# A DeepFM and CIN kernel: two more fields of tile 1 are looked up on chip in tile 0, and the last tile is transposed ahead of a layer of the tile before it

## What is computed

```python
emb = embed_table[f_ix, x_idx]                      # n, 26, 16
lin1 = w1_table[f_ix, x_idx].sum(axis=1, keepdims=True) + w1_bias
s = emb.sum(axis=1)
fm = 0.5 * ((s * s).sum(-1) - (emb * emb).sum(axis=(1, 2)))[:, None]
h = relu(emb.reshape(n, F * D) @ mlp_w1 + mlp_b1)
h = relu(h @ mlp_w2 + mlp_b2)
mlp_out = h @ mlp_w3 + mlp_b3
x0 = last = emb.transpose(0, 2, 1)
feats = []
for W in (cin_w0, cin_w1, cin_w2):
    last = einsum('ndl,ndf,klf->ndk', last, x0, W)
    feats.append(last)
cin = concatenate(feats, axis=-1).sum(axis=1) @ lin_w + lin_b
return lin1 + fm + mlp_out + cin
```

## Time and profile before

| | before |
|---|---|
| runs, us | 497.53, 497.66, 498.18 (median 497.66) |
| profiled execution, us | 496.48 |
| its span, us | 494.7 |
| mean granted clock of PE | 0.991 |
| busy share of the span | PE 92%, DVE 84%, ACT 74%, POOL 70% |
| gathers on POOL | 360 |
| look-ups | 56 |

### The profile page before, as it was taken

The page is one execution under the profiler, slowest core; times in us unless marked ns, Lnnn a source line. Parts: engine busy times, 40 slices in busy tenths (PEclk is TensorE's granted clock), DMA queues, the critical chain, the costliest instruction groups (busy, mean ns, idle before and its releaser), DMA issues.

```text
span 494.7 us, 6809 instructions
## 1 busy us (share of the span) xinstructions
PE 453.1 (92%) x2171; PEld 383.0 (77%) x2171; DVE 414.2 (84%) x861; ACT 368.2 (74%) x726; POOL 345.5 (70%) x365
## 2 busy tenths in 40 slices
PE   0988986899999999999999999999999999999898
PEld 0985764788888888888888888888877887878666
DVE  6163358999999999999999999999989989989676
ACT  0163499678787887888787878787887878687694
POOL 5777778777777777777777777777777777777000
PEclk9999998899999999999999999999999999999999
DMA  7963794222222222222222222222222222222000
GB/s 159 209 168 27 110 201 113 38 7 8 8 9 7 7 9 7 10 7 8 8 8 7 8 8 8 7 8 8 8 8 9 7 9 7 8 8 7 3 0 2
DMA packets 21522, 15.59 MB, mean 32 GB/s; under 512 B 12802, under 2 KB 19823, under 8 KB 21359
## 3 DMA queue, kind: packets, MB, share of 16 engines
q0 software_dynamic: 11520, 3.16, 18.6%
q1 hardware_dynamic: 6962, 9.99, 8.2%
q10 hardware_dynamic: 3005, 2.01, 2.0%
HBM read 14.92 MB, written 0.21 MB: 31 GB/s over the span
## 4 chain that ended last, share of the span: by engine, by line
POOL 65%; issue 22%; ACT 5%; PE 4%; DVE 3%; DMA 1%; POOLq 0%; DVEq 0%
POOL emb L499 65%; ACT ps_s L598 2%; ACT z_hi L591 2%; ACT z_hi L593 1%; DVE z_lo L796 1%; PE ps_q L1096 1%; PE ps_y L1127 1%; DVE xt L789 0%; DMA idx_raw<-x_idx 0%; PE ps_q L1097 0%; PE ps_q L1098 0%; DMA emb<-rows,idx_raw 0%; ACT room_a L597 0%; DVE sums L822 0%; DVE ps_y L935 0%
## 5 line engine op out<-in xcount | busy, mean ns | idle before, releaser
L499 POOL DMA_INDIRECT emb<-rows,idx_raw x360 | 345.1, 959 | 112.2 <-issue 109.4
L796 DVE TENSOR_TENSOR z_lo<-ps_s,z_hi 128x512 fp32r<-128x512 f32 (+1 forms) x192 | 131.4, 684 | 35.0 <-ACT ps_s L598 34.4
L591 ACT ACTIVATE z_hi<-ps_s 128x512 fp32r<-128x512 f32 (+1 forms) x192 | 114.4, 596 | 40.3 <-PE ps_s L1083 39.9
L598 ACT ACTIVATE ps_s<-ps_s 128x512 f32<-128x512 f32 (+1 forms) x192 | 113.9, 593 | 0.8
L1182 PE MATMUL ps_y<-look_hi,one_hot 128*128 128x442 f32 x224 | 82.1, 366 | 6.4 <-DVE one_hot L924 5.7
L1083 PE MATMUL ps_s<-xt,pick 128*128 128x512 f32 (+1 forms) x192 | 77.2, 405 | 9.3 <-ACT x_two L584 6.6
L1096 PE MATMUL ps_q<-z_lo,zw_hi 128*127 128x512 f32 (+1 forms) x192 | 79.6, 415 | 6.6 <-DVE z_lo L796 4.8
L1183 PE MATMUL ps_y<-look_lo,one_hot 128*128 128x442 f32 x224 | 79.4, 356 | 0.0
L1098 PE MATMUL ps_q<-z_hi,zw_hi 128*127 128x512 f32 (+1 forms) x192 | 75.9, 395 | 0.0
L1097 PE MATMUL ps_q<-z_hi,zw_lo 128*127 128x512 f32 (+1 forms) x192 | 75.8, 395 | 0.0
L1083 PEld LDWEIGHTS ps_s<-xt,pick 128*128 128x128 f32 (+1 forms) x192 | 35.6, 186 | 23.4 <-DVE z_lo L796 11.2
(11 more groups left out here) (187 smaller groups left out, 687.3 us busy)
## 6 DMA issues: line engine op xcount, KB each, us to landing
emb<-rows,idx_raw POOLq DMA_INDIRECT x360, 3.0
w_space<-rows SPq DMA_DIRECT2D x2, 728.9 KB
m_space<-rows SPq DMA_DIRECT2D x2, 728.9 KB
w_space<-key_scratch SPq DMA_DIRECT2D x1, 1408.0 KB, 8.6
w<-cin_w SPq DMA_DIRECT2D x2, 416.0 KB, 6.7
w<-cin_w ACTq DMA_DIRECT2D x2, 416.0 KB, 9.3
w_space<-cin_w SPq DMA_DIRECT2D x2, 416.0 KB, 8.4
w_space<-cin_w ACTq DMA_DIRECT2D x2, 416.0 KB, 8.2
```

The source lines that it names most:

```text
L499: pool.indirect_dma_start(emb[t % EMB][:, f, :], None, rows, bass.IndirectOffsetOnAxis(row_ix[:, t, f:f + 1], 0)).then_inc(gathered[t] if ...
L591: act.activation(z_hi[0:k, c, :], ps[0:k, :], ACT.Square)
L598: act.activation(ps[0:k, :], ps[0:k, :], ACT.Square).then_inc(hi_ready, 1)
L796: z = dve.tensor_tensor(z_lo[0:k, u % NC, :], ps, z_hi[0:k, u % NC, :].bitcast(F32), ALU.subtract)
```

## The change

Two of the empty slots are filled. Fields 22 and 23 of tile 1 are no longer gathered but looked up in slots 0 and 1 of tile 0 (`AHEAD = 2`), so tile 0 has four look-ups and tile 1 24 gathers. Tile 0 gets dictionaries of its own (`ROWS_0`, `KEYS_0`, `PICKED_0`), and the low parts of the tables are made one unit after the high ones in place of two. The copy of tile 1 waits for its two look-ups. The keys of tiles 1 and 2 come in with two loads. All later look-ups keep their slots.

Besides, `fold` moves from the end of `start_tile` to unit 4 of tiles 1 to 14, and `sum_products` from unit 3 to unit 6. In the step into tile 15, ACT makes the first part of the last copy ahead of the squares of unit 11; PE transposes ahead of the second layer of tile 14, and the eight filling matmuls go; DVE's `start_last` gets another order, in which the read of the second layer (`hidden2`) and `add_third` come behind unit 0 of tile 15. The diff, cut to what is spoken of; the parts belong, in order, to the constants, SP, POOL, ACT, DVE and PE:

```diff
-LATER = 2
+AHEAD = 2
...
-        key_first = sb("key_first", [P, LOOKS, P], F16)
+        key_first = sb("key_first", [P, AHEAD + LOOKS, P], F16)
...
         def looks(t):
-            return LOOKS if FIRST_LOOK <= t < T else 0
+            return LOOKS if FIRST_LOOK <= t < T else AHEAD if t == FIRST_LOOK - 1 else 0
 
         def look_no(t, i):
-            return LOOKS * (t - FIRST_LOOK) + i
+            return AHEAD + LOOKS * (t - FIRST_LOOK) + i if t >= FIRST_LOOK else i
 
         def look_at(t, slot):
-            n = LOOKS * t + slot - LATER
-            return (FIRST_LOOK + n // LOOKS, n % LOOKS) if 0 <= n < look_no(T, 0) else None
+            n = LOOKS * t + slot
+            if n < AHEAD:
+                return (FIRST_LOOK - 1, n)
+            m = n - AHEAD
+            return (FIRST_LOOK + m // LOOKS, m % LOOKS) if n < look_no(T, 0) else None
 
         def looked_by(t):
-            return min(max(LOOKS * t + 1 - LATER, 0), look_no(T, 0))
+            return min(LOOKS * t + 2, look_no(T, 0))
...
         ROWS = {0: 0, 3: 1, 6: 2, 9: 3}
         KEYS = {3: 1, 6: 2, 8: 3}
         PICKED = {3: 0, 6: 1, 9: 2}
+        ROWS_0 = {5: 0, 7: 1, 9: 2, 11: 3}
+        KEYS_0 = {3: 0, 5: 1, 7: 2, 9: 3}
+        PICKED_0 = {7: 0, 9: 1, 11: 2}
...
-        WARM, WARM_FIRST, WARM_LAST = 8, 4, (4, 4)
+        WARM, WARM_FIRST = 8, 4
...
-            sp.dma_start(key_first[:].rearrange("p i n -> p (i n)"),
-                         key_dram[LOOKS * FIRST_LOOK:LOOKS * (FIRST_LOOK + 1), :].rearrange(
-                             "r n -> (r n)").partition_broadcast(P)).then_inc(keys_first_in, 16)
+            for t, i0, i1 in ((FIRST_LOOK - 1, 0, AHEAD), (FIRST_LOOK, AHEAD, AHEAD + LOOKS)):
+                sp.dma_start(key_first[:, i0:i1, :].rearrange("p i n -> p (i n)"),
+                             key_dram[LOOKS * t:LOOKS * t + i1 - i0, :].rearrange(
+                                 "r n -> (r n)").partition_broadcast(P)).then_inc(keys_first_in, 16)
...
-                for f in range(F - looks(t)):
+                for f in [*range(F - LOOKS), *range(F - LOOKS + looks(t), F)]:
                     pool.indirect_dma_start(emb[t % EMB][:, f, :], None, rows,
...
                 if looks(t):
-                    act.wait_ge(looked, look_no(t, LOOKS))
+                    act.wait_ge(looked, look_no(t, looks(t)))
...
+                    if u == NU - 1 and t + 1 == T - 1:
+                        copy_last_early()
                     square(t, u)
                     if u == NU - 1 and t + 1 == T - 1:
-                        copy_last_early()
                         copy_last_late()
...
                     if u % NC == 2 and q:
                         add_product(t, q)
+                    if u == 4 and 0 < t < T - 1:
+                        fold(t - 1)
                     if u == 7:
                         hidden1_low(t)
-                    if t == 0 and u - 2 in LOOK_SPLIT:
-                        look_low(LOOK_SPLIT[u - 2])
-                    if u in PICKED and look_at(t, PICKED[u]):
-                        pick_row(*look_at(t, PICKED[u]))
-                    if u in KEYS and look_at(t, KEYS[u]):
-                        keys_to_one_hot(*look_at(t, KEYS[u]))
+                    slots = PICKED if t else PICKED_0
+                    if u in slots and look_at(t, slots[u]):
+                        pick_row(*look_at(t, slots[u]))
+                    if t == 0 and u - 1 in LOOK_SPLIT:
+                        look_low(LOOK_SPLIT[u - 1])
+                    slots = KEYS if t else KEYS_0
+                    if u in slots and look_at(t, slots[u]):
+                        keys_to_one_hot(*look_at(t, slots[u]))
 
             def start_last():
                 t = T - 1
+                times_third(t - 1)
                 times_left(t - 1, NQ - 1)
-                times_third(t - 1)
-                add_third(t - 1)
-                hidden2(t - 1)
                 x_low(t, 0)
                 x_low(t, 1)
                 z_low(t, 0)
+                hidden2(t - 1)
+                add_third(t - 1)
                 z_low(t, 1)
                 add_product(t - 1, NQ - 1)
                 z_low(t, 2)
...
                 add_product(t - 1, NQ - 1)
-                fold(t - 1)
...
-                    if u == 3 and t:
+                    if u == 6 and t:
                         sum_products(t - 1)
...
-                    if u in ROWS and look_at(t, ROWS[u]):
-                        look_rows(*look_at(t, ROWS[u]))
+                    slots = ROWS if t else ROWS_0
+                    if u in slots and look_at(t, slots[u]):
+                        look_rows(*look_at(t, slots[u]))
...
                 else:
+                    x_all(after)
                     hidden2(t)
-                    wait_for_bank(after, 1)
-                    free = s_bank(after, 0)
-                    keep_warm(free, WARM_LAST[0])
-                    x_all(after)
-                    keep_warm(free, WARM_LAST[1])
                     picked(after, 0)
                     picked(after, 1)
                     hidden1_whole(after)
```

More of the change, by code:

```diff
@@ L914, in keys_to_one_hot @@
             def keys_to_one_hot(t, i):
-                if i == 0 and t == FIRST_LOOK:
-                    dve.wait_ge(keys_first_in, 16)
+                if i == 0 and t == FIRST_LOOK - 1:
+                    dve.wait_ge(keys_first_in, 16 * 2)
                 elif i == 0 and t in (FIRST_LOOK + 1, FIRST_LOOK + 3):
@@ L919, in keys_to_one_hot @@
                 n = look_no(t, i)
-                keys = key_first[:, i:i + 1, :] if t == FIRST_LOOK else key_row[:, t - FIRST_LOOK - 1, i:i + 1, :]
+                keys = key_first[:, n:n + 1, :] if t <= FIRST_LOOK else key_row[:, t - FIRST_LOOK - 1, i:i + 1, :]
                 if n >= 2:
@@ L1173, in look_rows @@
                 n = look_no(t, i)
-                if n < LOOKS:
+                if t <= FIRST_LOOK:
                     pe.wait_ge(look_lo_ready, i + 1)
```

## The result

The changed kernel took 493.95 us (median of 4 runs, 493.86 to 494.42), the kernel before beside it 497.60 us (496.67 to 498.18): ratio 0.993, 95% interval 0.9917 to 0.9942. It is faster, by 0.3 to 0.7%, and both times lie under the predicted range of 495.9 to 501.0.

The account below looks back on a forecast made before the run. Two lines, DVE with ACT and POOL's gathers, were taken to bound the kernel, the later setting tile 14. Terms +0.2 - 0.1 + 1.2 = +1.3 us on the median 497.66 gave 498.9; range 495.9 to 501.0.

Parts of the forecast that it names:

- Tiles 1 to 13: Moving the fold and row sum in these tiles changes nothing: 0, bounds -0.05 and +0.05 us a tile.
- the compute line: DVE with ACT, setting the 26.34 us tile pace; predicted to bring tile 14's copy at 433.1, later than the gathers.
- by tile 14's copy: Start of tile 14's copy: +0.2 us against before, what the gathers save being spent in tile 0.
- the time from there to the end: From tile 14's copy on: -0.1 us for tile 14 and the last step together, +1.2 for the clock.
- putting the sum on a median: The +1.3 us sum was added to the median 497.66, not to the profiled execution of 496.48, giving 498.9.
- The gather line: POOL's gathers up to tile 14: two fewer, 2.5 us earlier; range 5.3 earlier to 0.3 later.
- Tile 0: Two added look-ups delay DVE's second x_low of tile 1 by 4.4 us, with stalls of 1.2 and 1.9; bounds +1.3, +7.3.
- the sign: Trace sign that the forecast is right: tile 2's copy starts near 117.0 us.
- Tile 14: PE no longer waits for comparisons behind the fold, so ACT's squares from unit 7 come 0.65 us earlier; bounds 0, -1.
- The step into tile 15: New order gains 2.2 us, lost again waiting for DVE's second-layer read; -0.1 us together with tile 14.
- The clock: PE's new 3.07 us gap before tile 15's first layer brings half clock: +1.2 us, range 0 to +2.4.
- Rival (2): Tile 0 takes the look-ups without the two stalls, +1.3; gathers decide tile 14, 2.5 us earlier: 496.3 us, chance 0.15.

Follow-up runs that it names:

- e1: Changed kernel with the fold and PE's row sum back at their old places: 498.27 us, ratio 1.0023 to the kernel before.
- e5: Changed kernel with the step into the last tile as in the kernel before, filling matmuls included: 493.38 us, ratio 0.9923 to the kernel before.
- e11: Changed kernel with the fold behind unit 3 in place of unit 4, row sum still at unit 6: 497.16 us, ratio 1.001 to the kernel before.
- e9: Changed kernel measured once more, nothing altered, as base for later runs: 495.39 us, ratio 0.9974 to the kernel before.
- e3: Changed kernel with the fold behind unit 3 and the row sum at unit 3: 497.31 us, ratio 0.9999 to the kernel before.
- e4: Changed kernel without the two look-ups of tile 1, the rest as changed: 498.77 us, ratio 1.0031 to the kernel before.
- e6: Changed kernel with DVE's read of tile 14's second layer ahead of unit 0 of tile 15: 491.82 us, ratio 0.9899 to the kernel before.
- e8: Changed kernel with four more reductions of the fold's input on DVE, unused, in tiles 3 and 4: 498.92 us, ratio 1.004 to the kernel before.
- e2: Changed kernel with the fold alone back at its old place, row sum at its new one: 499.91 us, ratio 1.006 to the kernel before.

## Why the prediction was wrong

**The step that failed is "Tiles 1 to 13", "I take 0, bounds -0.05 and +0.05 a tile".** Measured: -0.26 a tile. Its reason, "the same work stands between the same two waits", looked at DVE's two long waits alone. What was missing is that PE's comparisons stood behind the fold in every tile, not only in tile 14, where the prediction saw PE's idle 0.41 us for them and credited 0.65 us; and that a fold right behind its input starts 0.13 us late. About half of the 0.26 us is that start, the other half are DVE's short waits for ACT ahead of units 8 and 11, which the new place ends. Over the twelve tiles from copy 2 to copy 14 this is 3.1 us, and tile 1 gains 0.6 more: enough to turn which line comes later.

**The kernel nearest to the one that the prediction described is e1.** With the fold at its old place the compute line brings copy 14 at 434.10 without a wait (predicted 433.1). That its time of 498.27 us lies near the predicted 498.9 is partly luck: its first tiles came 1.3 us late, and its clock did not fall, for which the prediction had 1.2 us; the two about cancel.

**How the miss adds up.** The forecast was 5 us too high: 2.6 us by tile 14's copy (+0.2 predicted, -2.44 measured), 0.8 by the time from there to the end (+1.1 and +0.34), and 1.6 by putting the sum on a median that lay 1.2 us over the profiled execution before and 0.5 under it afterwards.

The other steps, one by one:
- The gather line, -2.5: it moved from 432.93 to 430.49, -2.44. That the number fits is partly luck. In it lie two things that nearly cancel: no gather of tile 0 takes 2.3 us any more in this execution (the longest 1.35), 1.4 us less in all, and the usual distance of two gathers is 1.258 us where it was 1.251, 1.6 us more in all. The first is a matter of the execution: e5 and e11, whose tile 0 is the same, have a gather of 2.79 us beside the third table split, the nine other profiles with the new tile 0 none over 1.35. The Trainium skill, SBUF — State Buffer, "Who interferes with whom", has a DVE instruction with two SBUF inputs contend with a GpSimd instruction that reads SBUF; the prediction took from it that all four table splits would stretch gathers. The runs have splits beside which a gather grew by 1.85 us and splits beside which none grew by more than 0.4 us, so as a fixed price for each split it does not hold here (lines below).
- Tile 0, +4.4: +4.79, with the two stalls of 1.2 and 1.9 us measured as 1.28 and 1.89. Tile 2's copy came at 116.04 all the same, where 117.0 was the sign: tile 0 began 0.8 us earlier in this execution, and tile 1 was 0.6 us shorter.
- Tile 14, -0.65: e5, which has the old step, shows 60.98 for the rest against 61.77, so -0.79.
- The step into tile 15, with tile 14 -0.1: -0.08 by e9 (61.69 against 61.77). The gap of 3.07 us is 2.75.
- The clock, +1.2: it is a matter of the execution, not of the kernel. Where the clock fell before the first layer (e3, e4), ACT waited 3.17 and 3.18 us for unit 2, where it stayed up (e9) 1.89: 1.28 us, so the size was right. The changed kernel's profiled execution lost 0.8 of it. The Trainium skill, TensorE: Matmul & The Clock Gate, "What's actually happening", has the half clock as the default that activity lifts; the prediction read from it a fall that is as good as sure, and the runs show it in four of eight profiles.
- Rival (2) has the right outcome, the gather line sets tile 14, but not its cause: tile 0 kept both stalls.

The stretched gather of e5 on POOL, and the split beside it on DVE:

```profile
81.80 2.79 POOL L506 DMA_INDIRECT emb<-rows,idx_raw  x1 [0.30 <-issue]
```
```profile
81.67 2.10 DVE L920 TENSOR_TENSOR look_lo<-m_space,look_hi 128x416 fp32r<-128x416 f32 x4
```

Profile to profile the gain is 2.1 us, median to median 3.65 and in the second measurement 1.6. Of the prediction's working, the chances don't add up as written: its parts give 0.41 for slower and 0.37 for the same, not 0.45 and 0.33; and two times carry 0.06 to 0.08 us that its terms don't give (96.45, 471.18). Nothing hangs on either.

## What to carry to other kernels

Where two lines run side by side, cost an edit by what each engine waits for in every repetition, not by the busiest engine's waits: an instruction that moves behind another engine's input is worth what of that engine's wait comes back to the line that sets the pace, times the tiles (here 0.4 us of PE's wait and 0.7 of ACT's gave 0.18 us a tile, e11 against e9). A wait noticed at the end of the loop is to be looked for in its middle. And a read that frees a bank for the next engine belongs into idle time ahead of it: one line moved (e6) gave 2.3 us between two profiles with the clock up.

## What was not expected of the hardware

- The clock behind a gap. Eight profiles (the changed kernel, e1 to e4, e8, e9, e11) have the same idle time of 2.75 or 2.76 us ahead of the first layer of tile 15. In four of them (the changed kernel, e3, e4, e8) PE then ran at a granted 0.50, in four at 1.00.
- The gathers' pace. With the fold at unit 4 two gathers stood 1.253 to 1.259 us apart (eight profiles, 100 to 200 and 300 to 400 us), with it elsewhere 1.249 to 1.252 (five, the kernel before among them). Over some 300 gathers that is 1.5 to 2 us on the gather line. Why was not tried.
- The start. ACT's copy for tile 1 came between 85.5 and 87.4 us in the kernels that are the same up to there. When the gather line leads, this need not reach the end, and when the compute line leads, it should. The spread of the times would fit in e6 (gathers lead, 491.55 to 492.35) and e11 (compute leads, 495.63 to 499.23), but not in e2 (compute leads, 499.32 to 500.58); it is not shown.
